# Last stage of a long-convolution and FFN kernel: y split in token order and turned by transposing DMAs instead of by PE

## What is computed

```python
xn = layernorm(x)
p  = (layernorm(xn) * gamma + beta) @ W_in + b_in      # v, x1, x2
y  = conv(v, k0) * x1
y  = conv(y, k1) * x2
attn = xn + y @ W_out + b_out                          # W_out is 256 x 256
ffn  = (silu(xn @ Wg.T) * (xn @ Wu.T)) @ Wd.T          # 768 hidden
out  = x + attn + ffn
```

## Time and profile before

| | |
|---|---|
| device time, median of 3 runs | 338.38 us (338.0 to 338.44) |
| span of the profiled execution | 336.8 us |
| own time of the profiled execution | not listed apart; the median is 1.6 us above the span |
| PE busy | 308.6 us, 92% |
| DVE busy | 258.0 us, 77% |
| ACT busy | 181.3 us, 54% |
| POOL busy | 214.0 us, 64% |
| last stage, from st_ready to the last finish | 299.2 to 332.3 us |

### The profile page before, as it was taken

The page is one execution under the profiler, slowest core; times in us unless marked ns, Lnnn a source line. Parts: engine busy times, 40 slices in busy tenths (PEclk is TensorE's granted clock), DMA queues, the critical chain, the costliest instruction groups (busy, mean ns, idle before and its releaser), DMA issues.

```text
span 336.8 us, 11903 instructions
## 1 busy us (share of the span) xinstructions
PE 308.6 (92%) x4945; PEld 240.1 (71%) x4945; DVE 258.0 (77%) x528; ACT 181.3 (54%) x389; POOL 214.0 (64%) x292
## 2 busy tenths in 40 slices
PE   0969897988989999999999999999999999989993
PEld 0439786976758776787777877777777866658992
DVE  2779999874586787686677779788786787978994
ACT  3636996753343544444553444443544434469991
POOL 6869879358878888677785858867777662200000
PEclk9999999999999999999999999999999999999999
DMA  7992044078859678786887868778687788101345
GB/s 230 340 365 65 2 140 175 10 252 306 358 198 377 212 313 298 262 370 225 342 293 280 368 232 334 270 286 339 244 368 247 306 337 332 40 1 65 125 149 168
DMA packets 21505, 81.01 MB, mean 241 GB/s; under 512 B 1478, under 2 KB 12618, under 8 KB 13258
## 3 DMA queue, kind: packets, MB, share of 16 engines
q1 hardware_dynamic: 19458, 77.47, 62.1%
q0 software_dynamic: 1840, 2.36, 2.4%
q10 hardware_dynamic: 152, 0.40, 0.4%
HBM read 75.50 MB, written 4.72 MB: 238 GB/s over the span
## 4 chain that ended last, share of the span: by engine, by line
PE 55%; DVE 18%; ACT 10%; POOL 7%; issue 6%; DMA 2%; POOLq 0%; DVEq 0%; SPq 0%; ACTq 0%
PE bank_c L300 13%; PE bank_p L300 13%; PE bank_u L300 9%; PE bank_d L300 9%; PE bank_g L300 9%; ACT vx L767 3%; ACT vx L759 3%; DVE sgh L983 2%; DMA bands<-in_L_attn_W_in 2%; DVE hhl L988 2%; DVE xT L819 2%; DVE stats L799 2%; DVE vx L840 1%; POOL ybuf L1298 1%; POOL res L1241 1%
## 5 line engine op out<-in xcount | busy, mean ns | idle before, releaser
L300 PE MATMUL bank_d<-wd,hhl 128*128 128x256 f16 x384 | 84.3, 271 | 0.4 <-DVE hhl L988 0.2
L300 PEld LDWEIGHTS bank_p<-wq,xT 128*128 128x128 f16 x1536 | 70.6, 99 | 16.9 <-issue 2.8
L300 PE MATMUL bank_p<-wq,xT 128*128 128x64 f16 x1536 | 80.0, 194 | 2.4 <-issue 2.4
L300 PE MATMUL bank_g<-xT,wgu 128*128 128x512 f16 x192 | 66.2, 378 | 0.7 <-ACT sgh L688 0.7
L300 PE MATMUL bank_u<-xT,wgu 128*128 128x512 f16 x192 | 66.2, 378 | 0.7 <-DVE sgh L983 0.7
L300 PEld LDWEIGHTS bank_c<-ybuf,bands 128*128 128x128 f16 x1024 | 51.9, 96 | 17.5 <-issue 0.9
L300 PEld LDWEIGHTS bank_c<-vhl,bands 128*128 128x128 f16 x1024 | 49.0, 96 | 20.8 <-issue 5.5
L300 PE MATMUL bank_c<-vhl,bands 128*128 128x64 f16 (+3 forms) x1024 | 57.3, 184 | 4.3 <-DVE ybuf L1004 1.9
L300 PE MATMUL bank_c<-ybuf,bands 128*128 128x64 f16 (+3 forms) x1024 | 60.3, 184 | 0.6 <-ACT ybuf L709 0.5
L694 ACT CAST hhl<-sgh 128x512 f16<-128x512 f32 x48 | 29.7, 618 | 50.6 <-DVE sgh L983 50.6
L1201 POOL TENSOR_TENSOR vx<-vx,bias 128x512 f32<-128x512 f32 x32 | 37.4, 1171 | 24.0 <-DVE vx L840 24.0
(11 more groups left out here) (191 smaller groups left out, 563.0 us busy)
## 6 DMA issues: line engine op xcount, KB each, us to landing
bands<-taps_seq SPq DMA_DIRECT2D x64, 1024.0 KB, 8.1
out<-res SPq DMA_DIRECT2D x8, 512.0 KB, 2.9
res<-in_L_attn_x SPq DMA_DIRECT2D x3, 1024.0 KB, 16.4
res<-in_L_attn_x SPq DMA_DIRECT2D x2, 512.0 KB, 6.2
bands<-in_L_attn_W_in SPq DMA_DIRECT2D x1, 768.0 KB, 6.2
bands<-in_L_ffn_w_gate POOLq DMA_DIRECT2D x1, 768.0 KB, 10.7
bands<-in_L_ffn_w_up POOLq DMA_DIRECT2D x1, 768.0 KB, 13.6
vx<-in_L_ffn_w_down POOLq DMA_DIRECT2D x1, 768.0 KB, 15.6
```

What stands on the lines that cost most here:

```text
L300: return nc.tensor.matmul(o, w, m, start=start, stop=stop, skip_group_check=True)
```

## The change

ACT writes the high half directly from the column of x1y2, scaled and rounded to fp16 in token order (`high_y`). DVE writes the low half with one scalar_tensor_tensor, column times scale minus high half (`low_y`). That pair serves 22 of the 32 blocks. The other 10 (every third, from block 2) are done by POOL alone with three linked instructions: scale to fp32, cast to the high half, subtract for the low half. The two halves lie side by side in a ring of 8 blocks (yhl) in half 0 of bands. SP turns each block with one transposing DMA, 128x512 fp16 into yT, also a ring of 8, once its low half is there; it waits for the block's old place in yT to be read. SP's 8 stores stand between those 32 DMAs. PE only projects, each block once its DMA has landed, and both transposes per block and the ACT rounding from PSUM are gone. The 4 output banks are now bank_c and bank_p, and DVE's `finish` follows its `low_y` six blocks later (three before).

```diff
--- before.py
+++ after.py
@@ -156,8 +156,12 @@
         xr = sb("xr", [P, 4, 4, P], F16)
         conv_lo = xr[:, :, :, :].rearrange("p r i t -> p (r i t)").bitcast(F32)[:, 0:2 * CH * NB].rearrange("p (h c b) -> p h c b", h=2, b=NB)
 
-        ysc = vx_flat[0][:, 0:4 * D].rearrange("p (r d) -> p r d", d=D)
-        yT = vx_flat[0][:, 4 * D:8 * D].bitcast(F16).rearrange("p (r i t) -> p r i t", r=4, i=4)
+        YR = 8
+        LOW = ("VVP" * NB)[:NB]
+        y_room = bands[:, 0, :, :, :].rearrange("p c e w -> p (c e w)")
+        yhl = y_room[:, 0:YR * 2 * D].rearrange("p (r n) -> p r n", r=YR)
+        yT = y_room[:, YR * 2 * D:2 * YR * 2 * D].rearrange("p (r i t) -> p r i t", r=YR, i=4)
+        y_alone = vx_flat[0][:, 0:2 * D].rearrange("p (r d) -> p r d", d=D)
 
 
         bank_g, bank_u = bank("bank_g"), bank("bank_u")
@@ -167,8 +171,7 @@
 
         x_bank = [bank_g, bank_u, bank_d[1]]
         w_bank = bank_d[0]
-        y_bank = [*bank_p, bank_g, bank_u]
-        o_bank = [*bank_c, *bank_d]
+        o_bank = [*bank_c, *bank_p]
         half = 3 * D // 2
 
 
@@ -203,8 +206,9 @@
             sem("gate_mm"), sem("up_mm"), sem("sg_ready"), sem("h_ready"), sem("hh_ready"), sem("hl_ready"),
             sem("down_mm"), sem("folded"))
         wo_max, wo_tp, wo_rm, wo_all, wo_ready = sem("wo_max"), sem("wo_tp"), sem("wo_rm"), sem("wo_all"), sem("wo_ready")
-        st_ready, ysc_ready, y_tp, yh_ready, yl_ready, out_mm, out_ready = (
-            sem("st_ready"), sem("ysc_ready"), sem("y_tp"), sem("yh_ready"), sem("yl_ready"), sem("out_mm"), sem("out_ready"))
+        st_ready, yh_ready, out_mm, out_ready = sem("st_ready"), sem("yh_ready"), sem("out_mm"), sem("out_ready")
+        yl_ready = {who: sem(f"yl_ready_{who}") for who in "VP"}
+        y_turned = [sem(f"y_turned{i}") for i in range(YR)]
         out_stored = sem("out_stored")
 
         def c(i, n=1):
@@ -289,9 +293,23 @@
                         sp.dma_start(bands[:, v, h * CH:(h + 1) * CH, :, :].rearrange("p c e w -> p (c e w)"), src).then_inc(band_loaded[v][h], 16)
 
             SB = 4
-            for i in range(NB // SB):
+
+            def turn_y(b):
+                sp.wait_ge(yl_ready[LOW[b]], nth(LOW, b, LOW[b]))
+                if b >= YR:
+                    sp.wait_ge(out_mm, b - YR + 1)
+                sp.dma_start_transpose(out=yT[:, b % YR, :, :], in_=yhl[:, b % YR, :]).then_inc(y_turned[b % YR], 16)
+
+            def store(i):
                 sp.wait_ge(out_ready, SB * i + SB)
                 sp.dma_start(out_v[:, SB * i:SB * (i + 1), :], res[:, SB * i:SB * (i + 1), :]).then_inc(out_stored, 16)
+
+            for b in range(NB):
+                turn_y(b)
+                if b >= SB + 6 - 1 and (b - 6 + 1) % SB == 0:
+                    store((b - 6 + 1) // SB - 1)
+            for i in range((NB - 6) // SB, NB // SB):
+                store(i)
             sp.wait_ge(out_stored, 16 * (NB // SB))
 
         @block.tensor
@@ -558,37 +576,21 @@
                     ffn_step(n, general)
                 for i in range(8):
                     down_part(STEPS - 2, i, general)
-                pe.wait_ge(wo_ready, 1)
-                pe.wait_ge(y2_ready, 2 * NG)
-                transpose_y(0)
-                transpose_y(1)
                 for i in range(8):
                     down_part(STEPS - 1, i, general)
-                for b in range(2, NB + 2):
-                    if b < NB:
-                        transpose_y(b)
-                    project_out(b - 2)
-
-            def transpose_y(b):
-                pe.wait_ge(ysc_ready, b + 1)
-                if b >= 4:
-                    pe.wait_ge(yl_ready, b - 3)
-                for k in range(KD):
-                    last = nc.tensor.transpose(y_bank[b % 4][:, k * P:(k + 1) * P], ysc[:, b % 4, k * P:(k + 1) * P], ident32[:, :])
-                last.then_inc(y_tp, 1)
+                pe.wait_ge(wo_ready, 1)
+                for b in range(NB):
+                    project_out(b)
 
             def project_out(b):
-                pe.wait_ge(yh_ready, b + 1)
-                pe.wait_ge(yl_ready, b + 1)
+                pe.wait_ge(y_turned[b % YR], 16 * (b // YR + 1))
                 if b >= 4:
                     pe.wait_ge(out_ready, b - 3)
-                elif b >= 2:
-                    pe.wait_ge(folded, 2 * NCHUNK - 3 + b)
                 o = o_bank[b % 4][:, 0:D]
                 n = 0
                 for e, f in ((0, 0), (1, 0), (0, 1)):
                     for k in range(KD):
-                        last = mm(o, yT[:, b % 4, 2 * e + k, :], wo[:, f, k, :], n == 0, n == 5)
+                        last = mm(o, yT[:, b % YR, 2 * e + k, :], wo[:, f, k, :], n == 0, n == 5)
                         n += 1
                 last.then_inc(out_mm, 1)
 
@@ -753,27 +755,19 @@
             round_h(STEPS - 2)
             silu(STEPS - 1)
 
-            def scale_y(b):
-                if b >= 4:
-                    act.wait_ge(y_tp, b - 3)
-                nc.scalar.activation(ysc[:, b % 4, :], x1y2[:, :, b:b + 1].rearrange("p c o -> p (c o)"), ACT.Copy,
-                                     scale=col(st[:, 0, :], b)).then_inc(ysc_ready, 1)
-
-            def round_y(b):
-                act.wait_ge(y_tp, b + 1)
-                if b >= 4:
-                    act.wait_ge(out_mm, b - 3)
-                o = y_bank[b % 4][:, 0:D]
-                nc.scalar.copy(yT[:, b % 4, 0:KD, :], o.rearrange("p (k t) -> p k t", k=KD)).then_inc(yh_ready, 1)
+            def high_y(b):
+                if b >= YR:
+                    act.wait_ge(y_turned[b % YR], 16 * (b // YR))
+                nc.scalar.activation(yhl[:, b % YR, 0:D], x1y2[:, :, b:b + 1].rearrange("p c o -> p (c o)"), ACT.Copy,
+                                     scale=col(st[:, 0, :], b)).then_inc(yh_ready, 1)
 
             act.wait_ge(st_ready, 1)
-            scale_y(0)
+            act.wait_ge(conv_mm[0], 2 * NG)
+            high_y(0)
             round_h(STEPS - 1)
-            scale_y(1)
-            for b in range(2, NB + 2):
-                if b < NB:
-                    scale_y(b)
-                round_y(b - 2)
+            for b in range(1, NB):
+                if LOW[b] == "V":
+                    high_y(b)
 
         @block.vector
         def _(dve):
@@ -1124,11 +1118,11 @@
             link(nc.vector.reciprocal(st[:, 1, :], st[:, 1, :]))
             split_h(STEPS - 1)
 
-            def split_y(b):
-                dve.wait_ge(yh_ready, b + 1)
-                o = y_bank[b % 4][:, 0:D]
-                nc.vector.tensor_tensor(yT[:, b % 4, KD:2 * KD, :], o.rearrange("p (k t) -> p k t", k=KD), yT[:, b % 4, 0:KD, :],
-                                        ALU.subtract).then_inc(yl_ready, 1)
+            def low_y(b):
+                dve.wait_ge(yh_ready, nth(LOW, b, "V"))
+                nc.vector.scalar_tensor_tensor(out=yhl[:, b % YR, D:2 * D], in0=x1y2[:, :, b:b + 1].rearrange("p c o -> p (c o)"),
+                                               scalar=col(st[:, 0, :], b), in1=yhl[:, b % YR, 0:D], op0=ALU.mult,
+                                               op1=ALU.subtract).then_inc(yl_ready["V"], 1)
 
             def finish(b):
                 dve.wait_ge(out_mm, b + 1)
@@ -1136,13 +1130,13 @@
                 nc.vector.scalar_tensor_tensor(out=res[:, b, :], in0=o, scalar=col(st[:, 1, :], b), in1=res[:, b, :],
                                                op0=ALU.mult, op1=ALU.add).then_inc(out_ready, 1)
 
-            for b in range(NB + 3):
-                if b < NB:
-                    split_y(b)
+            for b in range(NB + 6):
+                if b < NB and LOW[b] == "V":
+                    low_y(b)
                 if b == 1:
                     fold(NCHUNK - 1)
-                if b >= 3:
-                    finish(b - 3)
+                if b >= 6:
+                    finish(b - 6)
 
         @block.gpsimd
         def _(pool):
@@ -1321,6 +1315,24 @@
                 gate_2(G, 0)
                 gate_2(G, 1)
 
+            def split_y(b):
+
+                if b >= YR:
+                    pool.wait_ge(y_turned[b % YR], 16 * (b // YR))
+                if nth(LOW, b, "P") > 2:
+                    pool.wait_ge(yl_ready["P"], nth(LOW, b, "P") - 2)
+                y = y_alone[:, nth(LOW, b, "P") % 2, :]
+                high, low = (yhl[:, b % YR, e * D:(e + 1) * D] for e in range(2))
+                link(nc.gpsimd.tensor_scalar(y, x1y2[:, :, b:b + 1].rearrange("p c o -> p (c o)"), col(st[:, 0, :], b), None, ALU.mult))
+                link(nc.gpsimd.tensor_copy(high, y))
+                nc.gpsimd.tensor_tensor(low, y, high, ALU.subtract).then_inc(yl_ready["P"], 1)
+
+            pool.wait_ge(st_ready, 1)
+            pool.wait_ge(conv_mm[0], 2 * NG)
+            for b in range(NB):
+                if LOW[b] == "P":
+                    split_y(b)
+
 # ---- launch: one core; inputs and outputs as the reference has them ----
```

## The result

The changed kernel takes 360.41 us in the median of 4 runs (359.49 to 361.47), against 338.23 before (338.0 to 338.44): a ratio of 1.067, 95% interval 1.064 to 1.069. That is 22.2 us slower and outside the predicted range of 334.5 to 351. It is the second rival, at a price between its two values.

A forecast was written before the change was run, and what follows sets the result against it. ACT was taken to set the last stage's pace, 0.89 us a block, PE 0.87. Ten rounds of 2.71, then issue, landing, projection and finish, ended at 333.55 against 332.25: 338.38 + 1.3 = 339.7 us, range 334.5 to 351.

The forecast's parts named there:

- the second rival: SP's queue in the last stage: transposing DMAs cost 1.12 or 1.49 us each, giving 351 or 363 us; chance 0.28.
- I take the store's 0.37: SP in the last stage: issuing a transposing DMA of 128 KB takes 0.37 us, like a 512 KB store.
- threshold of 0.8: SP's queue: above 0.8 us per transposing DMA, the queue with its stores passes 0.89 us a block and decides.
- its formula: SP's queue: 32 x 1.12 + 7 x 0.37 = 38.4 us from 302.2, for transposing DMAs and stores.
- the estimate beside it: Turning a block by DMA: four 128x128 squares in a row, an estimated 5.2 us if nothing overlapped.
- Landing: Transposing DMA from issue to landing: 2.9 us, as for the store, with ends 1.7 and 4.6.
- The shared-port case: Last stage: DVE's low halves and POOL's instructions exclude each other, 0.90 us a block; 339.7 us, 335.7 to 345.9; chance 0.45.
- the reduction's ratio of 1.57: Cost of the column's stride, from DVE's reduction, 1.05 against 0.67 us; used for the upper end.
- ACT's ratio of 1.13: Cost of the column's stride, from ACT's scaling, 0.68 against 0.60 us; taken for DVE's low half and POOL's scaling.
- upper end of 0.88: POOL's scaling of a column in the last stage: 0.63 us taken, with ends 0.56 and 0.88.
- Rival one: Last stage: DVE and POOL hardly meet, a block's way through the DMA sets the pace; 335 us, faster; chance 0.27.
- price of 0.75: Pace per block in the last stage: six paces must cover 0.41 + 0.37 + 2.9 + 0.81 = 4.5 us, or 0.75.

The follow-up runs named there:

- The hybrids: Kernel before, with every third or every fourth block split by POOL and turned by one DMA: 336.31 and 338.48 us; with the DMA issued earlier: 336.87 and 336.51.
- plain copy: Changed kernel with its 32 transposing DMAs replaced by plain DMAs of the same 128 KB, y not turned: 341.03 us.
- halves: Changed kernel with each block turned by two transposing DMAs of 128x256 instead of one of 128x512: 400.15 us.
- a high half alone: Changed kernel with only the high half of each block turned, one transposing DMA of 128x256: 358.16 us.
- pairs: Changed kernel with two blocks turned by one transposing DMA of 128x1024, 16 DMAs in all: 346.17 us.
- the run with packed reads: Against the plain copy: ACT, DVE and POOL read 256 packed elements of W_out's tile instead of the column of y: 340.54 us.
- The plain copy with its stores last: Against the plain copy: all eight stores issued after the last copy: 346.86 us.

## Why the prediction was wrong

**What bounded the kernel before** was read rightly: ACT at 0.89 a block with PE at 0.87 behind it. The hybrids bear it out: with a quarter of the blocks off ACT, and their transposes off PE, the pace fell from 0.90 to PE's 0.82 once the DMA was issued early enough.

**The step that failed** is the term "I take the store's 0.37" for a transposing DMA on SP. It measured 1.22, and 1.5 behind a store, more than three times as much. The text had said that nothing in the trace bounds this price from above, and then took 0.37, by the row nearest in place, for the sum and for both of its ends; the kernel's trace held no transposing DMA at all. Rival two had the mechanism right. Its threshold of 0.8 wasn't tested, since the runs lie on both sides of it, at 0.46 to 0.57 for plain copies and at 1.2. With the measured prices its formula becomes 31 x 1.31 from start to start, and 1.0 for each of the six stores in between, where it counted seven (0.67 to the start of the next transpose, and 0.33 more for that one), which puts the last issue at 348.8; the trace has 349.6, and the one transpose that held SP for 2.2 is more than the difference. From that issue, 2.5 + 0.81 + 0.47 give 353.4, and the last finish ended at 353.54. What rival two had wrong was the form of the price: it counted squares of 128 by 128, while the runs with halves, a high half alone and pairs show a price per DMA, whatever its size from 64 to 256 KB. The chance of 0.28 and a range cut off at its middle, 351, left the result outside.

**The rule of the Trainium skill** (VectorE: DVE Perf Modes, The three transpose paths), 1309 ns for a 128x128 transpose by DMA against 390 on TensorE, spoke against the change and was right in direction. Its figure doesn't add up over four squares as the estimate beside it did: 128x512 landed 2.5 us after issue, and 128x1024 3.4. No run here has a single square by DMA. On PE the two squares of a block cost 0.21 us together in a row of them.

**Landing**, taken as 2.9, was 2.5 for the transpose, 3.5 right behind a store, and 2.1 for the plain copy; the ends of 1.7 and 4.6 held. That a square is written element by element is not what the trace shows: the transposes moved in packets of 256 bytes, where a store's are 1024. What the DMA engines pay for a turned block, an estimated 0.70 us against 0.39 for 128 KB of a store, had no term in the prediction. It cost nothing in the changed kernel, whose engines are not full.

**The shared-port case** can be judged on the plain copy, where SP's price is gone. It was forecast at 339.7 and came at 341.0, but two terms were mis-sized. It came near for a reason that was partly luck. The low half alone took 0.64, 1.56 times L1009's 0.41, and 0.55 to 0.57 from start to start where 0.40 was taken and 0.53 was the upper end. That it matches the reduction's ratio of 1.57 is chance: the packed read took 0.47, so the step is worth a third and something else the rest. ACT's ratio of 1.13 was misread, for it set half of two overlapping scalings (0.68) against the duration of one packed instruction (0.60). Duration against duration, it was 0.74 to 0.60, and the run with packed reads made it 0.74 to 0.51. POOL's scaling took 1.15, above the upper end of 0.88. The rule of the Trainium skill on GpSimd reads with a step over 8 bytes (GPSIMD Engine Reference, Performance pitfalls for Q7 kernels), half as much again, has the right sign; the packed read against the column shows 0.92 to 1.14, a quarter. What offset them is that DVE and POOL do not add up fully: 1.15 + 0.40 + 0.67 + 0.16 and two low halves at 0.57 would be 3.5 us for three blocks, and 2.70 was measured (3 x 0.90). The plain copy with its stores last shows each slowed by the other and both full, and the low halves fall into the two groups that the prediction named as its sign. So the contention is real, and its size was overdrawn: of the two low halves in a round only the one beside POOL's subtraction stood.

**Rival one**, a pace set by a block's way through the DMA, had a part in the plain copy: with stores between the copies it went at 0.97 a block in its steady part, and without them at 0.90. Its price of 0.75 left out that a copy behind a store lands after as much as 4.3 and not 2.1. For the pairs its part isn't shown, since their DMA engines were full.

**The signs named** for rival two came: a closed row on SPq, each DMA over 0.8, and PE, DVE, POOL and ACT waiting on it.

## What to carry to other kernels

A transposing DMA costs the issuing queue a fixed 1.2 us or so however much it turns, so count DMAs first: one per block of 0.89 us cannot keep up. Then count the DMA engines' time, by the estimate above 0.70 us for 128 KB turned: with its store a block needs 1.09, so grouping two blocks in one DMA doesn't keep up either (346.17 us). One in four blocks beside PE's own transposes gains. Where a trace lacks an operation altogether and one price for it would sink the change, that price belongs into the range, or a one-instruction measurement ahead of the design. Behind the first limit look for the second: here a plain copy, free of the transposing price, still left the kernel some 3 us slower than before.

## What the runs showed that was not expected

- SP is held by a transposing DMA for 1.18 to 1.23 us at least, for 64, 128 and 256 KB alike; a plain DMA of 128 KB holds it 0.46, and the store's 0.37 becomes 0.57 when it follows others closely. Where the DMA engines are full, plain stores hold it longer too: 1.3 us in the median of the eight in a row.
- The 16 DMA engines, nearly full or full, moved 177 GB/s of transposes and 343 GB/s of plain stores.
- POOL's tensor_scalar with one operation took 0.92 us for 256 packed elements, and L1241 with two operations 0.56. Why isn't settled.
- A DVE low half took 1.04 instead of 0.64 beside POOL's subtraction and 0.65 beside its scaling, while that scaling took 1.42 instead of 1.15: they slow each other, but by less than a full exclusion would.
